# One kernel, 32 samples: setup moved beside the first sample, one B and C projection for two branches, new instruction orders

## What is computed

```python
x = x + _L0_conv_ref(_gn(x), ...)   # mask from the centre of mass of each channel, relu, 3x3 convolution 256 to 256
x = x + _L1_conv_ref(_gn(x), ...)   # up by 2 with a 12 tap filter, bias, leaky relu, clamp at 256, down by 2
x = x + _L2_conv_ref(_gn(x), ...)   # projection to f1 and z; f2, f3 by 2x2 strided convolutions; four selective scans; gate; projection
x = x + _L3_conv_ref(_gn(x), ...)   # as L1, with its own filters and bias
```

## Time and profile before

| | us |
|---|---|
| median of 3 runs | 6593.88 |
| lowest and highest of them | 6589.45, 6598.32 |
| the profiled execution, its time | 6592.31 |
| its span, first to last instruction | 6590.5 |
| busy in it: TensorE | 5872.6 |
| busy in it: VectorE | 5785.4 |
| busy in it: ScalarE | 4123.9 |
| busy in it: GpSimd | 269.1 |
| mean granted clock of TensorE, share of 2.4 GHz | 0.935 |

### The profile page before, as it was taken

The page is one execution under the profiler, slowest core; times in us unless marked ns, Lnnn a source line. Parts: engine busy times, 40 slices in busy tenths (PEclk is TensorE's granted clock), DMA queues, the critical chain, the costliest instruction groups (busy, mean ns, idle before and its releaser), DMA issues. The chain is left out here.

```text
span 6590.5 us, 87758 instructions
## 1 busy us (share of the span) xinstructions
PE 5872.6 (89%) x32460; PEld 3815.8 (58%) x32460; DVE 5785.4 (88%) x4685; ACT 4123.9 (63%) x8002; POOL 269.1 (4%) x69
## 2 busy tenths in 40 slices
PE   5779999999999999999999999999999989999956
PEld 3445656655656655656655656655556655666634
DVE  1798889989899988989989899989899989899984
ACT  2556666666666666666666666666666666676654
POOL 0000000000000000000000000000000000000000
PEclk9889999999999999999999999999999999999978
DMA  1333323333333333323333333333333333333331
GB/s 41 92 92 85 102 81 105 98 86 89 96 86 105 98 83 92 99 82 106 98 82 93 95 88 105 98 85 90 97 87 104 98 87 88 101 85 102 98 83 41
DMA packets 332919, 597.12 MB, mean 91 GB/s; under 512 B 105718, under 2 KB 174526, under 8 KB 332362
## 3 DMA queue, kind: packets, MB, share of 16 engines
q1 hardware_dynamic: 332492, 591.50, 33.9%
HBM read 294.91 MB, written 58.81 MB: 54 GB/s over the span
## 5 line engine op out<-in xcount | busy, mean ns | idle before, releaser
L1209 DVE TENSOR_TENSOR_SCAN hb<-da,hb 128x1570 f32<-128x1570 f32 (+2 forms) x704 | 2332.7, 3343 | 6.1 <-ACT da L1020 2.2
L641 PE MATMUL ps<-pad,conv_w 128*128 128x392 f32 x4608 | 1563.9, 493 | 0.0
L641 PEld LDWEIGHTS ps<-pad,conv_w 128*128 128x128 f32 x4608 | 870.2, 189 | 660.7 <-issue 42.7
L691 PEld LDWEIGHTS ps<-down_k,ys 121*128 121x128 f32 x9216 | 1108.2, 193 | 205.7 <-DVE ys L1085 120.5
L691 PE MATMUL ps<-down_k,ys 121*128 121x121 f32 (+1 forms) x9216 | 1137.7, 276 | 83.0 <-DVE ys L1085 82.9
L672 PE MATMUL ps<-xt,up_k 123*121 123x256 f32 (+2 forms) x4096 | 1149.2, 426 | 6.6 <-ACT ys L920 6.3
L1224 DVE TENSOR_TENSOR hb<-hb,c_t 128x3136 f32<-128x3136 f32 (+1 forms) x384 | 1150.0, 3008 | 1.3
L1025 ACT ACTIVATE da<-delta_t,a_neg 128x784 f32<-128x784 f32 x1024 | 912.8, 940 | 316.3 <-DVE hb L1209 312.9
L1192 DVE TENSOR_TENSOR hb<-dx_t,b_t 128x3136 f32<-128x3136 f32 x256 | 880.4, 3439 | 49.6 <-PE ps L778 47.0
L920 ACT ACTIVATE ys<-ps 121x512 f32<-121x512 f32 x1152 | 670.2, 590 | 376.1 <-PE ps L672 246.6
L672 PEld LDWEIGHTS ps<-xt,up_k 123*121 123x121 f32 x4096 | 660.5, 192 | 330.3 <-ACT ys L920 159.8
(11 more groups left out here) (136 smaller groups left out, 5771.1 us busy)
## 6 DMA issues: line engine op xcount, KB each, us to landing
dx_t<-vc SPq DMA_DIRECT2D x256, 392.0 KB, 6.4
b_t<-scr SPq DMA_DIRECT2D x256, 392.0 KB, 4.1
delta_t<-vd SPq DMA_DIRECT2D x256, 392.0 KB, 6.9
c_t<-scr SPq DMA_DIRECT2D x256, 392.0 KB, 4.3
xa<-in_x SPq DMA_DIRECT2D x32, 784.0 KB, 4.4
xs<-xa SPq DMA_DIRECT2D x32, 784.0 KB, 3.3
xb<-xs SPq DMA_DIRECT2D x32, 784.0 KB, 5.5
out<-xb SPq DMA_DIRECT2D x32, 784.0 KB, 7.8
```

The source lines that it names most:

```text
L641: mm = nc.tensor.matmul(ps[:, half, 0:HALF], conv_w[:, c, tap, m * P:(m + 1) * P], pad[:, c, r0:r0 + HH // 2, tap % 3:tap % 3 + WW], start ...
L691: mm = nc.tensor.matmul(img(ps[:, reg, 0:17 * WW])[:, h + h0:h + h1, w + w0:w + w1], ys[0:KP, y % NY, at + n * P:at + (n + 1) * P], down_k ...
L1209: nc.vector.tensor_tensor_scan(h, a, b, 0.0, ALU.mult, ALU.add).then_inc(scan_done, 1)
```

## The change

Three things are changed together.

1. The setup block is gone. SP now starts with the load of x for sample 0, then eight early tensors (the group mean matrix, the identity, ramp, grid, conv_b, mask_w, filt and, last, conv_w), then all eight tap tiles into eight staging places, then the other 21 loads. TensorE waits for the early ones before its first step. VectorE makes small constants first, and the 64 products, the bias sum and the copies of the joined weights in front of its first clip. The six joining matmuls stand in front of the first turn on TensorE. The first `up` waits for all products, the first `f1` for all constants.
2. Branches 2 and 3 both read f1. Their B and C rows (32 each) come from one projection with 64 output rows, one copy and one write to `scr`. `bc.3`, `bce.3` and `bcw.3` are gone, and counters of 4 per sample become 3.
3. All five orders are new. The waits between the steps are the same, but for those that point 2 changes.

```diff
+                sp.dma_start(xa[:, :, :], sample(t["x"], 0)).then_inc(x_loaded, 16)
+                for dst, src in early:
+                    sp.dma_start(dst, src).then_inc(s_early, 16)
+                for n in range(4):
+                    for a in range(2):
+                        sp.dma_start(stage(n, a)[0:KP, :], t["taps"][n, a]).then_inc(s_stage, 16)
+                for dst, src in loads:
+                    sp.dma_start(dst, src).then_inc(s_load, 16)
...
+                    if s == 0 and p == FIRST and c == 0 and k == 0:
+                        combine()
...
+                    if s == 0 and u == 0:
+                        pe.wait_ge(s_kron, N_KRON)
...
+                    rows = 2 * N_STATE * (2 if q == 2 else 1)
...
+                    weights = bc_w[:, w:w + (2 if q == 2 else 1), :].rearrange("p w r -> p (w r)")
...
-                        mm = nc.tensor.matmul(out[0:2 * N_STATE, half, 0:n], bc_w[:, w, :], F[lev][:, half * HALF:half * HALF + n], start=True, stop=True)
+                        mm = nc.tensor.matmul(out[0:rows, half, 0:n], weights, F[lev][:, half * HALF:half * HALF + n], start=True, stop=True)
...
+                pe.wait_ge(s_early, 16 * len(early))
...
                 def clip(s, p, c, u):
                     y = N_UP * chunk_pass(p, s, c) + u
                     v = ys[0:KP, y % NY, :]
+                    if y == 0:
+                        weights()
```

The orders of TensorE, cut to the stretch of f1 and the last layer:

```diff
 PE_ORDER = """
-gm2.3@1 red.9@2 f1@1 f2@1 f3@1 bc.0@1 gm1.1@3 bc.1@1 gm1.0@0 bc.2@1 var.2@2 gm2.0@0 bc.3@1 z@1 red.10@2 gm2.1@3
-turn.0.0.0@3 turn.0.0.1@3 red.11@2 v.0@1 turn.0.0.2@3 turn.0.0.3@3 v.1@1 turn.0.1.0@3 up.0.0.0@3 up.0.0.1@3 up.0.0.2@3
-down.0.0.0@3 up.0.0.3@3 up.0.0.4@3 v.2@1 down.0.0.1@3 up.0.0.5@3 up.0.0.6@3 down.0.0.2@3 down.0.0.3@3 down.0.0.4@3
...
+cen.2@2 yi.3@2 gm1.3@1 var.2@2 gm2.3@1 f1@1 z@1 red.8@2 f2@1 gm2.1@3 f3@1 bc.0@1 red.9@2 turn.0.0.0@3 turn.0.0.1@3
+bc.1@1 turn.0.0.2@3 turn.0.0.3@3 bc.2@1 turn.0.1.0@3 up.0.0.0@3 up.0.0.1@3 up.0.0.2@3 v.0@1 up.0.0.3@3 up.0.0.4@3
+down.0.0.0@3 down.0.0.1@3 down.0.0.2@3 up.0.0.5@3 up.0.0.6@3 v.1@1 down.0.0.3@3 gm1.0@0 down.0.0.4@3 up.0.0.7@3
+up.0.0.8@3 down.0.0.5@3 turn.0.1.1@3 turn.0.1.2@3 down.0.0.6@3 turn.0.1.3@3 gm2.0@0 down.0.0.7@3 red.10@2 up.0.1.0@3
...
```

Those of VectorE around the same place:

```diff
 DVE_ORDER = """
...
-fin.1.1.0@1 fin.1.1.1@1 mix.1.2@2 hc.9@2 db.8@2 sc.10.0@2 sc.10.1@2 db.9@2 hc.10@2 sc.11.0@2 sc.11.1@2 mr.0.0@0
-hc.11@2 mr.1.0@0 mix.1.3@2 mr.0.1@0 mix.2.0@2 mr.1.1@0 ms@0 mc@0 clip.0.0.0@3 sp1.0@1 sp2.0@1 sp3.0@1 sp4.0@1 mb@0
-mix.2.1@2 mm.0@0 mx.0@0 clip.0.0.1@3 mm.1@0 clip.0.0.2@3 sp1.1@1 sp2.1@1 sp3.1@1 sp4.1@1 clip.0.0.3@3 clip.0.0.4@3
-db.0@1 mx.1@0 mix.2.2@2 sc.0.0@1 clip.0.0.5@3 clip.0.0.6@3 hc.0@1 sc.1.0@1 hc.1@1 clip.0.0.7@3 sp1.2@1 clip.0.0.8@3
...
+sc.9.0@2 sc.9.1@2 hc.9@2 db.8@2 db.9@2 sc.10.0@2 clip.0.0.0@3 clip.0.0.1@3 mix.2.0@2 clip.0.0.2@3 clip.0.0.3@3
+sc.10.1@2 clip.0.0.4@3 clip.0.0.5@3 sp1.0@1 hc.10@2 clip.0.0.6@3 clip.0.0.7@3 sp2.0@1 clip.0.0.8@3 sp3.0@1 sc.11.0@2
+sp4.0@1 sc.11.1@2 clip.0.1.0@3 fin.0.0.0@3 fin.0.0.1@3 clip.0.1.1@3 clip.0.1.2@3 hc.11@2 clip.0.1.3@3 mr.0.0@0
+clip.0.1.4@3 mr.1.0@0 mr.0.1@0 sp1.1@1 mr.1.1@0 ms@0 clip.0.1.5@3 clip.0.1.6@3 sp2.1@1 mc@0 db.0@1 mb@0 sp3.1@1 mm.0@0
+clip.0.1.7@3 mx.0@0 sp4.1@1 clip.0.1.8@3 sc.0.0@1 mix.2.1@2 mix.2.2@2 fin.0.1.0@3 fin.0.1.1@3 mm.1@0 hc.0@1 sc.1.0@1
...
+db.4@1 db.5@1 sc.6.0@1 clip.1.0.0@0 clip.1.0.1@0 sc.6.1@1 clip.1.0.2@0 clip.1.0.3@0 hc.6@1 clip.1.0.4@0 clip.1.0.5@0
+sp1.3@1 sp2.3@1 clip.1.0.6@0 clip.1.0.7@0 sp3.3@1 clip.1.0.8@0 sp4.3@1 sc.7.0@1 sc.7.1@1
```

More of the change, by code:

```diff
@@ L96 @@
[L96 to L100, removed]
@@ new lines @@
+bo.0@2 conv.1.0@0 bo.1@2 conv.1.1@0 conv.1.2@0 conv.1.3@0 cen.0@1 conv.1.4@0 conv.1.5@0 conv.2.0@0 var.0@1 red.2@1
+conv.2.1@0 red.3@1 conv.2.2@0 conv.2.3@0 conv.2.4@0 conv.2.5@0 cen.1@1 conv.3.0@0 conv.3.1@0 conv.3.2@0 conv.3.3@0
+conv.3.4@0 conv.3.5@0 var.1@1 gm1.1@2 gm1.2@0 yi.2@1 red.4@1 gm2.2@0 v.3@1 red.5@1 turn.1.0.0@0 turn.1.0.1@0
+turn.1.0.2@0 turn.1.0.3@0 turn.1.1.0@0 turn.1.1.1@0 up.1.0.0@0 up.1.0.1@0 up.1.0.2@0 up.1.0.3@0 down.1.0.0@0
+down.1.0.1@0 up.1.0.4@0 up.1.0.5@0 down.1.0.2@0 down.1.0.3@0 up.1.0.6@0 up.1.0.7@0 down.1.0.4@0 up.1.0.8@0
@@ L609, in take_bank, with combine @@
                         pe.wait_ge(*bank_free[reg][i - 1])
+                def combine():
+                    pe.wait_ge(s_load, 16 * len(loads))
+                    for w in range(3):
+                        nc.tensor.matmul(ps[:, 6, w * P:(w + 1) * P], raw_dt[:, 2 * w * P:(2 * w + 1) * P],
+                                         raw_dt[:, (2 * w + 1) * P:(2 * w + 2) * P], start=True, stop=True).then_inc(s_comb, 1)
+                    for c in range(NC):
+                        nc.tensor.matmul(ps[:, 7, c * P:(c + 1) * P], raw_in[:, c * P:(c + 1) * P], raw_c1,
+                                         start=True, stop=True).then_inc(s_comb, 1)
+                    nc.tensor.matmul(ps[:, 7, NC * P:NC * P + 1], raw_c1, in_b[:, 0:1], start=True, stop=True).then_inc(s_comb, 1)
                 def gm1(s, k):
@@ L998, in bce @@
                         act.wait_ge(scr_written, 16 * i)
-                    nc.scalar.copy(wide(bcr[0:2 * N_STATE, :], n), wide_ps(slot[0:2 * N_STATE, :, :], n)).then_inc(bc_copied, 1)
+                    nc.scalar.copy(wide(bcr[0:rows, :], n), wide_ps(slot[0:rows, :, :], n)).then_inc(bc_copied, 1)
                 def da_of(s, u, *p):
@@ L1005, in da_of @@
                     part = p[0] if p else 0
+                    if s == 0 and u == 0:
+                        act.wait_ge(s_exp, 2)
                     if u >= 3:
@@ L1080, in _, with constants @@
             def _(dve):
+                def constants():
+                    nc.vector.memset(zero[:, :], 0.0).then_inc(s_set, 1)
+                    nc.vector.memset(cst[:, 0:1], GN_EPS).then_inc(s_set, 1)
+                    nc.vector.memset(cst[:, 1:2], LN_EPS).then_inc(s_set, 1)
+                    nc.vector.memset(cst[:, 2:3], -(3.0 ** 0.5) / 4.0).then_inc(s_set, 1)
+                    nc.vector.memset(cst[:, 3:4], -SERIES_UNTIL).then_inc(s_set, 1)
+                    dve.wait_ge(s_early, 16 * len(early))
+                    nc.vector.tensor_scalar(filt[:, :], filt[:, :], 1.0, -1.0, ALU.is_equal, ALU.mult).then_inc(s_set, 1)
+                    dve.wait_ge(s_set, 6)
+                    nc.vector.tensor_tensor(neg_mw[:, :], neg_mw[:, :], filt[:, :], ALU.mult).then_inc(s_set, 1)
```

196 lines of the change are left out of this document (91 added, 105 removed).

## The result

The changed kernel takes 6168.8 us (median of 4 runs, 6161.6 to 6171.2), the kernel before 6591.7 us (6588.4 to 6598.3): ratio 0.9355, 95% interval 0.9339 to 0.9372. The forecast was 6262 us with a range of 6110 to 6440 us; the time lies inside it and 93 us under the forecast.

A forecast was written before the change was run, and what follows sets the result against it. VectorE and TensorE each work about 180 of 197.5 us per sample, the rest being waits of both. 6592.3 - 41 (start) - 3 (fill) - 263 (orders) - 24 (tail) = 6261; forecast 6262 us, range 6110 to 6440.

The forecast's parts named there:

- Start, -41 us: Setup beside the first sample: first statistic matmul at about 14 us instead of 54.8, a gain of 41 us (35 to 43).
- The -3 us of the fill: Before the first scan: z moves ahead of f2 and one slot turn of 2.4 us goes, -3 us with rounding.
- Joined projection: One B and C projection of 64 rows for two of 32: matmul cost taken 0, gain 0 to 2.4 us per sample.
- part 3: The new engine orders: VectorE's work stays 180 us per sample, waits shrink to 9 us, -263 us over 31 rounds (-450 to 0).
- Orders, 197.5 to 189 us: Sample period under the new lists: 180 us of VectorE work plus 9 us of waits, -8.5 us; ends 183 and 197.5.
- The two holes: VectorE's idle 6.17 us at the last layer's first clip and 3.46 us at branch 1's softplus, claimed to go.
- four tight handovers: Handovers between engines with slack under 1 us; a failing one costs 1 to 2 us, 7 us per sample allowed.
- The clock, which was given as a rule against: TensorE waits about 3.4 us ahead of f1; at 1.2 GHz f1 and z take 5.3 us more, 3 us per sample reaching VectorE.
- rival A: TensorE or its clock takes the waits' place: 194 to 195 us per sample, 6431 us; chance 0.13.
- Tail, -24 us: After the last scan: output projection of sample 31 starts near 30 us instead of 54, a gain of 24 us (10 to 28).
- Rival C: Nine clips ahead of sc.11.0 wait for a late ScalarE step and VectorE stands still: slower, 6664 us; chance 0.04.
- rival D: The orders run at their work, 182 to 183 us per sample: 6059 us; chance 0.05.

## Why the prediction came out as it did

- **Start, -41 us:** measured 41.0 (13.81 for the forecast's 14). The products are hidden, and their price in the open was right too (12.8 us). The -3 us of the fill did not come: the first scan moved by exactly what the first matmul moved by. Under the old orders they are there (first matmul to first scan 157.8 us, for 160.6 before and 160.5 in the changed kernel), so the joining gave them and the new orders took them back.
- **Joined projection, counted inside part 3 with ends at 0 and 2.4 us per sample:** the 64 rows cost nothing, as put. The slot's chain was named rightly (1.50 us and a wait). It was worth 2.8 us under the old orders and 2.2 under the new, so this end of the range was the truth, and past it by 0.4. The step that failed here is to price a dropped ScalarE copy at its own 0.80 us: the norm and the mask stood behind it.
- **Orders, 197.5 to 189 us:** measured 185.8. The work of 180 us was right (180.3). The two holes were gone as said. The term of 7 us for four tight handovers was mis-sized. The waits of a sample are 4.99 us in all, and 2.36 with TensorE's gaps filled; the period is then 183.0 us, the lower end that the sum of the lists had given. So the sum made by hand was good to a microsecond, though its holes lie elsewhere, and the allowance on top of it stands for next to nothing. Of the handovers named, scan 9.0 waits 0.32 us for "about 1", all clips together wait 0.6 us a sample, and red.2 and red.3 end 0.46 and 0.17 us ahead of db.2 and db.3, for 0.4 and 0.3; red.2 fails as soon as VectorE comes 1 us earlier. Not foreseen were the distances (1.2 to 1.6 us) and da.8.0.
- **The clock, which was given as a rule against:** the gap is 3.30 us for "about 3.4", and f1 falls to the lower level. z does not, so f1 and z take 2.1 us more and not 5.3. With f1 alone made warm 52 us come back, 1.7 us per sample, for "3". The path to VectorE was another too: not red.9 and db.9, but da.7.1, which stands behind f1's copy in ScalarE's list. A second slow place, at red.9, was not foreseen; with it the clock costs 2.6 us per sample. That is rival A's mechanism, present, but on top of 183 us and not of 189. The forecast's own sum held nothing for it.
- **Tail, -24 us:** measured 24.8, and by the path named: the output projection of sample 31 starts at 6107.56 us, 28 us after the last scan, for "near 30".
- **Rival C** (the nine clips ahead of the scan 11.0 hold VectorE up) did not happen: VectorE's waits for clips are 0.8 and 0.9 us in the two samples above. The clips put back behind the scan were not tried.

In sum: the forecast stood 6 us per sample above the lists' own 183. The truth stood 2.8 above it, and nearly all of that was the clock. Over the 31 rounds between the first and the last scan the forecast was a gain of 8.5 us each, and 356.5 / 31 = 11.5 came: 93 us, which is what the forecast was too high by; the other terms were off by 3 us or less. Part of the nearness is luck. The allowance was some 6 us per sample too much and the clock's 2.6 us were left out, so two errors of opposite sign stood in one term; without the clock the time is 6089.9 us, outside the range and near rival D.

## What to carry to other kernels

Price a removed step by what stands behind it in its queue, not by its own length: a copy of 0.8 us was worth 2 to 3 us a sample. When orders are made anew so that an engine waits in front of a large matmul group, look at the granted clock of that group, and fill the gap with matmuls into an accumulator that is overwritten anyway. And where work summed along the new lists leaves few holes, price each handover that looks tight by itself; a flat allowance on top was the one large error here, and a cost that was worked out but kept out of the sum, the clock's, hid part of it.

## What the runs showed of the hardware

- TensorE's gaps below 0.5 us can matter. Behind three gaps of 0.36, 0.48 and 0.31 us the granted clock was 0.60 in the window shown and red.9 took over 1.75 us in 19 of 30 samples, and in none once three short matmuls filled them. One gap of 1.92 us made z slow in 9 of 30 samples, where with a gap of 1.00 us it was slow in none of the changed kernel's. The Trainium skill, TensorE: Matmul & The Clock Gate, Part 1, has two states that activity switches; the levels agree (0.50 in the window of the cold f1, 1.00 in that of the fast red.9), and which sample falls is not told by its own work, which was the same in both samples shown.
- A GpSimd multiply of two tensors and a VectorE scan of two tensors did not run side by side here. The multiply began at 3193.15, inside the first of two scans (3190.63 to 3194.05), and ended at 3195.70; the pair of scans took 8.36 for 6.74 us. That fits a multiply of 1.6 us that waits for the first scan and is waited for by the second. In the changed kernel 31 such scans took 5.0 us where the others took 3.4; without the multiply on GpSimd none took over 3.43. The Trainium skill, SBUF — State Buffer, Who interferes with whom, calls the port that the two engines share an exclusive lock; the trace agrees. On VectorE the same multiply takes 0.95 us, so GpSimd relieved VectorE of nothing: its two steps cost VectorE 2.24 us and take 1.52 there.
